# Choosing each token's expert inside the attention loop, and a DRAM list of token numbers in place of a table made at its end

## The chip, the cores and the metric

The kernel runs on one core of one Trainium2 chip. The metric is the device time in microseconds of one execution. A time of 1403.3 us is the median of three runs of the kernel before; the profile is of one more execution.

## What is computed

Eight batches of 512 tokens with 256 channels go through three steps: a cross-attention with 16 heads on 64 context rows, of which each token keeps the 32 highest scores per head; a self-attention with 16 heads of 16 channels; and a feed-forward layer in which each token uses one of eight experts, the one with the highest gate logit. Cut to what the change touches, the last step is:

```python
hn2 = _layernorm(x, ln2_g, ln2_b).reshape(-1, h)
logits = hn2 @ gate_w + gate_b
idx = jnp.argmax(logits, axis=-1)                 # one expert of 8 for each of 4096 tokens
mid = jax.nn.relu(jnp.einsum('th,ehf->etf', hn2, w1) + b1[:, None, :])
y = jnp.einsum('etf,efh->eth', mid, w2) + b2[:, None, :]
moe = y[idx, jnp.arange(hn2.shape[0])]
return x + moe.reshape(b, s, h)
```

## The kernel before

**Two blocks.** The first block is the attention of all eight batches, each in four tiles of 128 tokens (`NT = 4`, `TILES = 32` in all). The second is the routing and the experts: the tokens are sorted by expert into 39 tiles of 128 (`ETILES`), enough for any split of 4096 tokens over eight experts. Between the blocks all engines meet at a barrier.

**The order in the first block.** Each engine's work is written as many small streams (one function for each step of a batch, a tile or a group of heads). `weave` puts the streams of an engine into one order by their due times, which `due(b, kind, n)` works out from the table `AT`: a kind of step, its times within a batch, stretched and shifted for each batch. Batches overlap; the gate of batch b ends while the heads of batch b+1 run. The eight PSUM banks are handed out in the same way: a step that writes an `fr` bank (four of them) takes the next turn in `FR_TURN`, and its turn waits until the reader of the turn four before it is done.

**The places named below.** TensorE's matmuls all go through the helper at L613, its transposes through L616. VectorE finds a bound of each row's scores at L1244 (`nmax`, from scores in `fr` and what ScalarE left in `over`); TensorE transposes `nmax` (`fr<-ident,nmax`, kind `ct`), and ScalarE's exponentials (`pt<-fr`, L1013) follow on scores `fr<-qs,ks`. For the top 32 of the cross-attention VectorE builds `nhi`, `lo`, `merged` and `thr` and the mask `m` (L1180); GpSimd multiplies it with the exponentials (`m<-m,e`, L1358), adds halves, VectorE sums (L1187) and inverts (`rden`, L1201), GpSimd scales (`m<-m,rden`, L1372), and TensorE transposes the product (`xs<-ident,m`). GpSimd also adds a bias (`xy<-xy,bo_b`, L1395) and writes the normalised rows (`row<-xyf,z`, L1413), which go to the DRAM list `rows_d`. The gate is four matmuls for a tile (`fr<-gw,znT`) and VectorE's sum into `logits` (L1293).

**The second block.** The SP queue loads constants (`dcon`, L1472). VectorE then finds the best expert of all 32 tiles at once (L1488 to L1493); two matmuls (L1592, L1593) count the tokens ahead of each; VectorE adds up over the tiles, finds the tile in which each expert begins, each token's slot, and for each slot its tile and row (L1497 to L1551), all on 128 partitions; 32 matmuls (L1628) bring the token numbers into the order of the slots. From `rec` VectorE copies three index columns for each tile into `gix`: the token rows, the weight rows and the `b2` rows. GpSimd fetches by them with indirect DMAs (L1662), two tiles ahead: `rows`, `w1s`, `w2s` and `b2s`. A tile is then two transposes (L1599), 32 matmuls of layer one (L1609), 16 of layer two (L1621), and an indirect DMA of the result (L1700). Weights of an expert that is already in the buffer are not fetched again: their index lies outside the bound.

Of the kernel before, what the change touches and what calls it, by code (L numbers as in the profile page):

```python
# [13 lines left out]
P = 128  # L14
# [21 lines left out]
for _name, _n in (("temp", HP), ("ln1_g", KT), ("ln1_b", KT), ("bq", KT), ("bk", KT), ("bv", KT),  # L36
# [157 lines left out]
FR_TURN = turns("proj", "v", "fs", "ct", "st", "ot", "oT", "wo", "zT", "gt")  # L194
# [28 lines left out]

DCON = {}
for _name, _n in (("before", P), ("ones", P), ("order", E), ("steps", TILES), ("starts", SEGS + 1),
                  ("tile", ETILES), ("row", P), ("part", 1), ("token", TILES)):
    DCON[_name] = sum(n for _, n in DCON.values()), _n
# [8 lines left out]
def program(nc, x, ctxT, maskb, wqT, wk, wv, wo, cols, fwq, fwk, fwv, fwo, bo, gate_w, gate_b,  # L236
            w1b, w2t, b2, ident_in, dcon_in, out):
    ctx = ExitStack()
    with ctx:
# [18 lines left out]
        rows_d = dram("rows_d", (TOK + 1, 2 * DM))  # L258

# [4 lines left out]
        mask_u = sb("mask_u", [P, B * CK], U8)  # L264
# [6 lines left out]
        logits = sb("logits", [P, TILES * E])  # L271
        zrow = sb("zrow", [NT * 4, P])

        def cv(name, n):
            return col[:, COLS[name][0] + n:COLS[name][0] + n + 1]

# [65 lines left out]
        row = sa("row", [P, 2, 2 * DM])  # L342
        znT = sa("znT", [P, KT, P])


        pre_ctx = pt[:, 0, 0:KT, :]
# [46 lines left out]
        rows_stored, scratch_set = [sem(f"rows_stored{n}") for n in range(2)], sem("scratch_set")  # L393

        dcon_loaded = sem("dcon_loaded")
        d_step, oh_ready, count_full, counts_read = sem("d_step"), sem("oh_ready"), sem("count_full"), sem("counts_read")
        rows_ready, tokens_full, rec_ready = sem("rows_ready"), sem("tokens_full"), sem("rec_ready")
# [4 lines left out]
        gix_ready = pair("gix_ready")  # L402
        rows_in, w1_in, w2_in, b2_in = pair("rows_in"), pair("w1_in"), pair("w2_in"), pair("b2_in")
# [44 lines left out]
        def _(sp):  # L448
# [13 lines left out]
            load(mask_u[:, :], maskb.to_broadcast((P, B * CK)), early_loaded)  # L462
# [8 lines left out]
            load(gb_b[:, :], gate_b.to_broadcast((P, E)), const_loaded)  # L471

# [138 lines left out]
        def _(pe):  # L611
# [240 lines left out]
            def gate(b, t):  # L852
# [3 lines left out]
                for k in range(KT):  # L856
                    ins = mm(o[:, 0:E], znT[:, k, :], gw[:, k, :], k == 0, k == KT - 1)
                ins.then_inc(fr_full, 1)

            weave([first_values(), context()]  # L860
                  + [part(b) for b in range(B) for part in (fold_k, fold_v, projections, values)]
# [7 lines left out]
        def _(act):  # L869
# [170 lines left out]
            def out_turned(b, t):  # L1040
                yield due(b, "to", t)
                fr_written(act, b, "oT", t)
                for k in range(KT):
# [410 lines left out]
        def dc(name):  # L1454
            a, n = DCON[name]
            return dcon[:, a:a + n]
# [296 lines left out]
```

## Time and profile before

| | us |
|---|---|
| median of three runs | 1403.3 (1400.73 to 1408.4) |
| the profiled execution | 1396.75 |
| its span, first to last instruction | 1394.9 |
| TensorE busy | 1283.2 (92%) |
| VectorE busy | 942.8 (68%) |
| ScalarE busy | 854.2 (61%) |
| GpSimd busy | 682.3 (49%) |

The busy shares are means over two different blocks, so they tell little by themselves. The attention fills the span up to some 1052 us, the routing the next 37 us, the expert tiles the rest. How full an engine is where a step is to be added is read from the busy time of short stretches, what a step waits for from the timeline.

### The profile page before, as it was taken

Reading aid. Unit: us, or ns where it says so; the run is one execution under the profiler, and the core shown is the slowest. Engines: PE = TensorE matmul, PEld = TensorE weight load, DVE = VectorE, ACT = ScalarE, POOL = GpSimd, SP = SyncE. Lnnn points to the kernel's source line nnn. Section 1 sums busy time; section 2 is a strip of 40 time slices with the busy share of each in tenths; the row PEclk is TensorE's granted clock in tenths of the full one; section 3 lists DMA queues with packets and bytes.
Section 4 is the critical chain, followed back from the end, with each engine's and each line's share of the span. In section 5 each row is a group of like instructions: output and inputs, shape, how many; then the busy total and the mean of one; then the engine's idle time right before and its main releaser. Section 6 shows DMA issues by size and latency. Waiting matters only on the chain. (4 is left out here: it accounts for less than half of the span.)

```text
span 1394.9 us, 27066 instructions
## 1 busy us (share of the span) xinstructions
PE 1283.2 (92%) x7138; PEld 922.0 (66%) x7138; DVE 942.8 (68%) x6185; ACT 854.2 (61%) x2061; POOL 682.3 (49%) x816
## 2 busy tenths in 40 slices
PE   7868799999999999999999999999972899999996
PEld 5445576577576566656757666655531799989996
DVE  3887987996997998799699789944426122222221
ACT  2334488697878879779787887977860122222221
POOL 2557453555356355445624734632013466666673
PEclk9989999999999999999999999999995899999998
DMA  5210641743363184175337417418513264385551
GB/s 189 83 62 9 167 93 31 169 99 77 101 154 82 55 181 93 40 154 121 77 91 155 91 33 196 78 49 195 93 46 136 77 221 152 82 303 187 188 193 26
DMA packets 105009, 161.43 MB, mean 116 GB/s; under 512 B 35058, under 2 KB 58232, under 8 KB 100760
## 3 DMA queue, kind: packets, MB, share of 16 engines
q1 hardware_dynamic: 86760, 106.51, 32.7%
q0 software_dynamic: 18096, 53.19, 11.7%
q8 instruction: 58, 0.95, 0.3%
q14 instruction: 95, 0.78, 0.2%
HBM read 161.81 MB, written 46.53 MB: 149 GB/s over the span
## 5 line engine op out<-in xcount | busy, mean ns | idle before, releaser
L1013 ACT ACTIVATE pt<-fr 128x512 f32<-128x512 f32 x512 | 277.1, 617 | 25.7 <-PE fr L613 22.6
L1244 DVE CUSTOM_DVE_ANT_0 over<-fr,over 128x256 f32<-128x256 f32 x512 | 197.8, 418 | 86.7 <-ACT over L1023 79.2
L1023 ACT ACTIVATE over<-fr 128x256 f32<-128x256 f32 x512 | 179.0, 391 | 53.4 <-PE fr L613 49.0
L613 PE MATMUL fr<-qs,ks 128*128 128x512 f32 x512 | 189.1, 452 | 3.8 <-DMA qs<-cT 1.3
L613 PE MATMUL fr<-ks,qs 128*128 128x256 f32 x512 | 170.7, 352 | 8.1 <-DVE nmax L1244 3.9
L1358 POOL TENSOR_TENSOR m<-m,e 128x1024 f32<-128x1024 f32 x32 | 75.9, 2371 | 185.0 <-DVE m L1180 185.0
L613 PEld LDWEIGHTS fr<-qs,ks 128*128 128x128 f32 x512 | 87.1, 188 | 86.5 <-issue 50.5
L613 PE MATMUL fr<-kd,qs 128*128 128x256 f32 x512 | 137.5, 283 | 0.0
L814 PE MATMUL ob<-pt,v 128*32 128x512 f32 x1024 | 136.4, 604 | 0.6 <-ACT pt L1013 0.5
L613 PEld LDWEIGHTS fr<-ks,qs 128*128 128x128 f32 x512 | 97.8, 191 | 43.9 <-DVE nmax L1244 25.0
L613 PE MATMUL xs<-VW,pT 128*128 128x256 f32 x512 | 120.2, 389 | 1.8 <-issue 1.7
L613 PE MATMUL xs<-M,xnT 128*128 128x512 f32 x256 | 120.3, 592 | 0.2 <-ACT xnT L872 0.2
L613 PEld LDWEIGHTS xs<-VW,pT 128*128 128x128 f32 x512 | 98.9, 196 | 16.2 <-issue 2.3
L613 PEld LDWEIGHTS fr<-kd,qs 128*128 128x128 f32 x512 | 98.4, 192 | 8.0 <-issue 4.8
L1350 POOL TENSOR_TENSOR e<-s,mx 128x1024 f32<-128x1024 f32 x32 | 60.9, 1904 | 62.5 <-issue 36.9
L1157 DVE MAX8 lo<-lo 128x8 f32<-128x32 f32 x512 | 90.3, 177 | 0.0
L1151 DVE MAX8 lo<-lo 128x8 f32<-128x32 f32 x512 | 89.8, 176 | 0.0
L1158 DVE MAX8 nh<-nhi 128x8 f32<-128x32 f32 x512 | 89.6, 175 | 0.0
L1152 DVE MAX8 nh<-nhi 128x8 f32<-128x32 f32 x512 | 89.3, 175 | 0.0
L1155 DVE MATCH_REPLACE8 nhi<-nh,nhi 128x32 f32<-128x32 f32 x512 | 89.0, 174 | 0.0
L1154 DVE MATCH_REPLACE8 lo<-lo 128x32 f32<-128x32 f32 x512 | 88.8, 174 | 0.0
L1372 POOL TENSOR_TENSOR m<-m,rden 128x1024 f32<-128x1024 f32 x32 | 60.9, 1905 | 47.2 <-DVE rden L1201 47.2
(211 smaller groups left out, 2903.9 us busy)
## 6 DMA issues: line engine op xcount, KB each, us to landing
parts_d<-parts SPq DMA_DIRECT2D x32, 512.0 KB, 4.2
ks<-parts_d SPq DMA_DIRECT2D x128, 128.0 KB, 4.0
qs<-parts_d SPq DMA_DIRECT2D x128, 128.0 KB, 4.3
xy_d<-xy SPq DMA_DIRECT2D x32, 256.0 KB, 3.9
kd<-diff_d SPq DMA_DIRECT2D x128, 64.0 KB, 4.1
xyf<-xy_d SPq DMA_DIRECT2D x32, 256.0 KB, 4.0
rows_d<-row SPq DMA_DIRECT2D x32, 256.0 KB, 3.3
diff_d<-diff SPq DMA_DIRECT2D x16, 256.0 KB, 2.3
```

The source lines that it names most:

```text
L613: return pe.matmul(o, l, r, start=first, stop=last)
L814: ins = pe.matmul(ob[VC * h:VC * h + VC, :], v32[:, t, 4 * g + h, :], pt[:, t % 2, h, :], start=(t == 0), stop=(t == NT - 1))
L1013: act.activation(pt[:, t % 2, h, :], fr_bank(b, "st", 16 * g + n)[:, :], ACT.Exp, scale=D ** -0.5)\
L1023: act.activation(over[:, (16 * g + n + 64 * b) % NREL, :], fr_bank(b, "fs", 16 * g + n)[:, S // 2:S], ACT.Relu)\
L1151: v.max(lo17[:, h, 1:9], lv[:, h, :])
L1152: ins = v.max(nh17[:, h, 0:8], nv[:, h, :])
L1154: v.match_replace(lv[:, h, :], lo17[:, h, 1:9], lv[:, h, :], -BIG)
L1155: ins = v.match_replace(nv[:, h, :], nh17[:, h, 0:8], nv[:, h, :], -BIG)
L1157: v.max(lo17[:, h, 9:17], lv[:, h, :])
L1158: ins = v.max(nh17[:, h, 8:16], nv[:, h, :])
L1244: v.tensor_tensor_reduce(rest, fr_bank(b, "fs", 16 * g + n)[:, 0:S // 2], rest, 1.0, -BIG, ALU.add, ALU.max, nmax[:, g % 2, 4 * h + t:4 * ...
L1358: gp.tensor_tensor(m[:, :, :], m[:, :, :], e[:, :, :], ALU.mult).then_inc(em_ready, 1)
```

## The change

**Choice and count, batch by batch.** `choose` finds the expert of the batch's 512 tokens once their logits are there (ties go to the lower number), in five steps on 128x32; `places` has TensorE count by five matmuls the tokens of the same expert ahead of each token: in the tile, in earlier tiles of the batch, and in earlier batches (`acc`); `count` adds the batch to `acc`; `slots` picks each token's place, as an integer. Each expert owns a region of 4096 places in the list. `ids_out` scatters the token numbers of a tile to their places in a DRAM list `ids_d`, with an indirect DMA of 128 numbers of 4 bytes, four for each batch. The list is filled with the number 4096 (no token) ahead of time.

**The second block.** It counts on 8 partitions how many tiles each expert needs, makes a table of 39 tiles by matmuls, and one indirect DMA fetches the 39 rows of 128 token numbers. One transpose turns them into `row_table`; `w_table` holds the weight rows. GpSimd's DMAs take their indices from the two tables, so that the copies into `gix` and `sid` go. `b2` stands behind the rows of `w2` (2304 words), so that the `b2` DMA goes. The first tile is always of expert 0, and its weights are plain loads on the SP queue at the block's start. The sum with the residual rows (`resb`) moves on VectorE behind the middle layer. The constants are loaded in the prologue.

The new kinds in the table, and the new streams (`mm` is the matmul helper, `fr_slot` takes the bank's turn):

```diff
+    "ch": (331.237,),
+    "dp": (333.413,),
+    "cn": (333.871,),
+    "sx": (335.219,),
+    "ro": (338.117, 339.873, 341.639, 343.291),
-FR_TURN = turns("proj", "v", "fs", "ct", "st", "ot", "oT", "wo", "zT", "gt")
+FR_TURN = turns("proj", "v", "fs", "ct", "st", "ot", "oT", "wo", "zT", "gt", "dp")
...
+            def places(b):
+                yield due(b, "dp")
...
+                pe.wait_ge(oh_ready, b + 1)
+                wait(pe, acc_ready, b)
+                o = fr_slot(b, "dp", 0)
+                chosen_here = oh[:, :, :].rearrange("p t e -> p (t e)")
+                mm(o[:, 0:NT * E], earlier[:, :], chosen_here, True, False)
+                mm(o[:, 0:NT * E].rearrange("p (t e) -> p t e", e=E), ones[:, :],
+                   acc[:, b % 2, :].unsqueeze(1).to_broadcast((P, NT, E)), False, False)
+                for back in range(1, NT):
+                    ins = mm(o[:, back * E:NT * E], ones[:, :], chosen_here[:, 0:(NT - back) * E], False, back == NT - 1)
+                ins.then_inc(fr_full, 1)
...
+            def set_picks():
+                yield due(0, "nx", 0) - 0.01
+                dve.wait_ge(dcon_loaded, 16 * 3)
+                v.tensor_copy(earlier[:, :], oT[:, 0, :])
+                v.tensor_copy(ones[:, :], oT[:, 1, :])
+                v.tensor_copy(acc[:, 0, :], znT[:, 0, 0:E]).then_inc(pick_set, 1)
+
+            def choose(b):
+                yield due(b, "ch")
...
+                v.tensor_reduce(best[:, :], logits[:, :, :], AX.X, ALU.max).then_inc(choice_step, 1)
+                dve.wait_ge(choice_step, 4 * b + 1)
+                v.tensor_tensor(ow[:, :, :], logits[:, :, :], best[:, :].unsqueeze(2).to_broadcast(wide), ALU.is_ge)\
+                 .then_inc(choice_step, 1)
...
+                v.tensor_tensor(oh[:, :, :], ow[:, :, :], best[:, :].unsqueeze(2).to_broadcast(wide), ALU.is_equal)\
+                 .then_inc(oh_ready, 1)
...
+            def slots(b):
+                yield due(b, "sx")
+                fr_written(dve, b, "dp", 0)
+                v.tensor_tensor(ow[:, :, :], fr_bank(b, "dp", 0)[:, 0:NT * E].rearrange("p (t e) -> p t e", e=E),
+                                oh[:, :, :].bitcast(F32), ALU.mult).then_inc(fr_signal(b, "dp", 0), 1)
...
+            def ids_out(b):
+                for t in range(NT):
+                    yield due(b, "ro", t)
...
+                    if t == 0:
+                        pool.wait_ge(slots_ready, b + 1)
+                    pool.sem_inc(p_gate, 1)
+                    gp.indirect_dma_start(ids_d.rearrange("r (p o) -> (r p) o", o=1),
+                                          bass.IndirectOffsetOnAxis(slot_i[:, t:t + 1], 0),
+                                          dc("token")[:, b * NT + t:b * NT + t + 1], None,
+                                          bounds_check=E * REGION - 1, oob_is_err=False).then_inc(ids_stored, 16)
```

The second block, cut to its core:

```diff
-            sp.dma_start(dcon[:, :], dcon_in).then_inc(dcon_loaded, 16)
+            sp.dma_start(w1s[:, 0, :], w1b[0:P, :]).then_inc(first_w1, 16)
+            sp.dma_start(w2s[:, 0, :], w2t[0:P, :]).then_inc(first_w2, 16)
...
+            settle(v.tensor_scalar(cnt[:, :], counts_at[:, 0:1], of_expert("region"), None, ALU.subtract))
+            settle(v.tensor_scalar(more_than[:, :], of_expert("steps"), cnt[:, 0:1], None, ALU.is_lt))
+            v.tensor_reduce(need[:, :], more_than[:, :], AX.X, ALU.add).then_inc(need_ready, 1)
...
+            dve.wait_ge(table_full, 1)
+            v.tensor_scalar(ids_at[:, :], begins_at, 1.0 / P, dc("part")[0:ETILES, :], ALU.mult, ALU.add)\
+             .then_inc(ids_at_ready, 1)
...
+            dve.wait_ge(ids_full, 1)
+            v.tensor_copy(row_table[:, :], ids_t).then_inc(ids_ready, 1)
...
+            pe.transpose(ids_t, ids[:, :], ident[0:ETILES, 0:ETILES]).then_inc(ids_full, 1)
...
-            for t in range(TILES):
-                if t % 8 == 0:
-                    pe.wait_ge(rows_ready, t // 8 + 1)
-                ins = pe.matmul(EO[1][:, 0:SEGS], at_row[:, t, :], at_tile[:, t, :], start=(t == 0),
-                                stop=(t == TILES - 1))
...
-            for q in range(2):
-                pool.wait_ge(gix_ready[q], 1)
-                fetch_w1(0, q)
-                fetch_w2(0, q)
+            pool.wait_ge(ids_at_ready, 1)
+            pool.wait_ge(ids_stored, 16 * TILES)
+            gather(ids[:, :], ids_d, ids_at[:, :], ids_in, RTILES - 1)
+            pool.wait_ge(tables_ready, 1)
+            fetch_w1(0, 1)
+            pool.wait_ge(ids_ready, 1)
             for q in range(2):
                 fetch_rows(0, q)
+            fetch_w2(0, 1)
```

**Where the new steps stand.** On TensorE, where the gate of batch 0 has just ended; `xs<-kbd,wqT_s` is a fold of keys, `ob<-pt,v` the values under the exponentials. Before:

```order
L613 MATMUL fr<-kd,qs 128x256
L613 MATMUL fr<-qs,ks 128x512 x3
L613 MATMUL xs<-kbd,wqT_s 128x128 x4
L616 MATMUL fr<-ident,nmax 16x128
L613 MATMUL fr<-qs,ks 128x512 x4
L814 MATMUL ob<-pt,v 32x512 x4
```

After:

```order
L645 MATMUL fr<-kd,qs 128x256
L645 MATMUL fr<-qs,ks 128x512 x3
L645 MATMUL xs<-kbd,wqT_s 128x128 x4
L648 MATMUL fr<-ident,nmax 16x128
L645 MATMUL fr<-oh,earlier 128x32
L645 MATMUL fr<-acc,ones 128x32
L645 MATMUL fr<-oh,ones 128x24
L645 MATMUL fr<-oh,ones 128x16
L645 MATMUL fr<-oh,ones 128x8
L645 MATMUL fr<-qs,ks 128x512 x4
L846 MATMUL ob<-pt,v 32x512 x4
```

The five counting matmuls stand between the transpose of `nmax` and the next scores for ScalarE.

On VectorE at the same place; `ISA` is the top-key step that gives `nmax`. Before:

```order
L1121 SCALAR_TENSOR_TENSOR nhi<-s,nb 128x512
L1244 ISA over,nmax<-fr,over 128x256
L1244 ISA nmax 128x1
L1172 TENSOR_REDUCE thr<-merged 128x16
L1128 TENSOR_TENSOR lo<-s 128x512
L1180 TENSOR_TENSOR m<-s,thr 128x1024
```

After:

```order
L1170 SCALAR_TENSOR_TENSOR nhi<-s,nb 128x512
L1358 TENSOR_REDUCE best<-logits 128x4
L1360 TENSOR_TENSOR ow<-logits,best 128x32
L1363 TENSOR_TENSOR ow<-ow,dcon 128x32
L1366 TENSOR_REDUCE best<-ow 128x4
L1371 TENSOR_TENSOR oh<-ow,best 128x32
L1293 ISA over,nmax<-fr,over 128x256
L1293 ISA nmax 128x1
L1221 TENSOR_REDUCE thr<-merged 128x16
L1378 TENSOR_REDUCE tsum<-oh 128x8
L1381 TENSOR_TENSOR acc<-acc,tsum 128x8
L1177 TENSOR_TENSOR lo<-s 128x512
```

The choice's five steps stand ahead of that step, the count's two ahead of `lo`; the slots' three steps and then `m` follow. (Batches 3 and 5 have the choice ahead of `nhi`, batch 2 the slots ahead of `lo`.)

On GpSimd, behind batch 0's gate. Before:

```order
L1350 TENSOR_TENSOR e<-s,mx 128x1024
L1413 TENSOR_TENSOR row<-xyf,z 128x256
L1372 TENSOR_TENSOR m<-m,rden 128x1024
L1395 TENSOR_TENSOR xy<-xy,bo_b 128x256
L1358 TENSOR_TENSOR m<-m,e 128x1024
L1364 TENSOR_TENSOR e<-e 128x16x32
L1366 TENSOR_TENSOR e<-m 128x16x32
```

After:

```order
L1449 TENSOR_TENSOR e<-s,mx 128x1024
L1512 TENSOR_TENSOR row<-xyf,z 128x256
L1524 DMA ids_d<-dcon,slot_i 37760x1
L1471 TENSOR_TENSOR m<-m,rden 128x1024
L1524 DMA ids_d<-dcon,slot_i 37760x1
L1494 TENSOR_TENSOR xy<-xy,bo_b 128x256
L1524 DMA ids_d<-dcon,slot_i 37760x1 x2
L1457 TENSOR_TENSOR m<-m,e 128x1024
L1463 TENSOR_TENSOR e<-e 128x16x32
```

The four scatters stand around `m<-m,rden` and ahead of the next `m<-m,e`; batches 1 to 5 read alike. Batch 6's four stand together between two pairs of `row` steps, batch 7's behind its last `row`, ahead of the barrier.

At the end of the first block on GpSimd, from the last `row` over the barrier (the branches). Before:

```order
L1413 TENSOR_TENSOR row<-xyf,z 128x256 x2
L1422 UNCONDITIONAL_BRANCH
L1656 UNCONDITIONAL_BRANCH
L1662 DMA w1s<-w1b,gix 128x2056
L1662 DMA w2s<-w2t,gix 128x2048
L1662 DMA b2s<-b,gix 128x256
L1662 DMA w1s<-w1b,gix 128x2056
```

After:

```order
L1512 TENSOR_TENSOR row<-xyf,z 128x256 x2
L1524 DMA ids_d<-dcon,slot_i 37760x1 x4
L1535 UNCONDITIONAL_BRANCH
L1718 UNCONDITIONAL_BRANCH
L1724 DMA ids<-ids_d,ids_at 39x128
L1724 DMA w1s<-w1b,w_table 128x2056
L1724 DMA rows<-rows_d,row_table 128x512 x2
L1724 DMA w2s<-w2t,w_table 128x2304
```

Four scatters stand ahead of the barrier, and behind it the fetch of the token numbers comes first.

## Rows read from the trace of the kernel before

**Rows 1.** By stretch: length; busy PE, PEld, DVE, ACT, POOL; granted clock, DMA.
```profile
297.70:306.00 8.30, 8.30 (x54) 5.27 (x53) 8.30 (x56) 7.98 (x19) 7.60 (x10) 1.00 0.63 90
306.00:317.80 11.80, 11.80 (x73) 7.49 (x72) 11.13 (x97) 11.08 (x23) 6.12 (x5) 1.00 0.36 65
1052.50:1077.00 24.50, 2.07 (x4) 1.17 (x4) 18.74 (x50) 0.00 (x0) 7.88 (x5) 0.50 0.32 107
```

**Rows 2.** Timeline of the gap: start us, length us, engine, operation, [idle before].
```profile
1051.71 0.17 DVE L1293 TENSOR_TENSOR logits<-fr,gb_b 128x8 f32<-128x8 f32 x1 [2.07 <-PE fr L613]
1052.17 0.34 SPq L1472 DMA_DIRECT2D dcon<-dcon_in  x1
...
1072.63 0.19 DVE L1545 SCALAR_TENSOR_TENSOR best<-best,slot 128x32 f32<-128x32 f32 x1
1072.86 0.35 DVE L1546 TENSOR_SCALAR best<-best 128x32 f32<-128x32 f32 x1
...
1084.87 0.21 DVE L1557 TENSOR_SCALAR gix<-rec 128x1 uint32<-128x1 f32 x2
1085.88 1.00 POOL L1662 DMA_INDIRECT rows<-rows_d,gix  x1 [7.45 <-DVE gix L1557]
...
1089.29 0.69 PE L1599 MATMUL fr<-ident,rows 128*128 128x128 f32 x2 [4.71 <-DMA rows<-rows_d,gix]
```

**Rows 3.** Timeline of the loop, where the gate of batch 0 ends.
```profile
297.06 0.51 PE L613 MATMUL fr<-gw,znT 128*128 128x8 f32 x4
...
299.12 1.05 PE L613 MATMUL xs<-kbd,wqT_s 128*128 128x128 f32 x8
...
299.55 0.08 DVE L1244 DVE_READ_ACCUMULATOR2_ANT nmax<- 128x1 f32 x1
...
300.01 0.27 PE L616 MATMUL fr<-ident,nmax 128*16 128x128 f32 x1
```

**Rows 4.** Timeline of the gap, GpSimd's first six indirect DMAs.
```profile
1067.90 1.36 POOL L1662 DMA_INDIRECT w1s<-w1b,gix  x1 [18.36 <-issue]
...
1069.57 2.34 POOL L1662 DMA_INDIRECT w2s<-w2t,gix  x1 [0.31 <-issue]
...
1072.21 1.01 POOL L1662 DMA_INDIRECT b2s<-b,gix  x1 [0.30 <-issue]
...
1073.52 2.07 POOL L1662 DMA_INDIRECT w1s<-w1b,gix  x1 [0.30 <-issue]
...
1075.89 1.22 POOL L1662 DMA_INDIRECT w2s<-w2t,gix  x1 [0.30 <-issue]
...
1077.42 1.00 POOL L1662 DMA_INDIRECT b2s<-b,gix  x1 [0.30 <-issue]
```

**Rows 5.** Expert tiles: chain of waits; last, TensorE's waits (us, times, longest).
```profile
1090.88 5.47 PE xs L1609 x32
...
1100.02 3.57 PE fr L1609 x32
...
1127.51 5.67 DMA rows<-rows_d,gix
...
PE fr L1599 <- DMA rows<-rows_d,gix: 5.1, 5, 1.5
```

**Rows 6.** Timeline of GpSimd, and last of VectorE, behind batch 0's gate.
```profile
310.99 0.73 POOL L1413 TENSOR_TENSOR row<-xyf,z 128x256 f32<-128x256 f32 x1
312.59 1.90 POOL L1372 TENSOR_TENSOR m<-m,rden 128x1024 f32<-128x1024 f32 x1 [0.87 <-DVE rden L1201]
314.45 0.73 POOL L1395 TENSOR_TENSOR xy<-xy,bo_b 128x256 f32<-128x256 f32 x1
319.14 2.38 POOL L1358 TENSOR_TENSOR m<-m,e 128x1024 f32<-128x1024 f32 x1 [3.95 <-DVE m L1180]
...
324.26 1.22 DVE L1187 TENSOR_REDUCE sums<-e 128x32 f32<-128x1024 f32 x1 [2.62 <-POOL e L1366]
```

**Rows 7.** Waits from 297.7 to 414.7: us in total, times, longest.
```profile
PEld xs L616 <- POOL m L1372: 1.1, 2, 0.9
```

More of the change, by code:

```diff
@@ L221 @@
 W1COLS = KT * FF + FT
+REGION = TOK
+RTILES = E * REGION // P + ETILES
+W2COLS = FT * DM + DM
 DCON = {}
-for _name, _n in (("before", P), ("ones", P), ("order", E), ("steps", TILES), ("starts", SEGS + 1),
-                  ("tile", ETILES), ("row", P), ("part", 1), ("token", TILES)):
+for _name, _n in (("order", E), ("token", TILES), ("part", 1), ("upto", E), ("steps", TILES),
+                  ("tile", ETILES), ("bump", 1), ("region", 1), ("expert", 1)):
     DCON[_name] = sum(n for _, n in DCON.values()), _n
@@ L270, in program @@
         gw = sb("gw", [P, KT, E])
-        logits = sb("logits", [P, TILES * E])
+        dcon = sb("dcon", [P, NDCON])
+        earlier = sb("earlier", [P, P], F32R)
+        ones = sb("ones", [P, P], F32R)
+        acc = sb("acc", [P, 2, E], F32R)
         zrow = sb("zrow", [NT * 4, P])
@@ L1042, in out_turned @@
                 fr_written(act, b, "oT", t)
+                if b == 0 and t == 0:
+                    act.wait_ge(pick_set, 1)
                 for k in range(KT):
@@ L1298, in _ @@
+            weave([place_keys(), set_picks()]
+                  + [part(b) for b in range(B) for part in (x_stats, parts_low, choose, count, slots)]
                   + [part(b, t) for b in range(B) for t in range(NT)
@@ L1554, in _, with of_expert @@
[L1554 to L1565 removed]
+            def of_expert(name):
+                return dc(name)[0:E, :]
@@ new lines, in _ @@
+            settle(v.tensor_tensor(begins[:, :], starts_at, need[:, :], ALU.subtract))
+            v.tensor_scalar(weigh[:, :], begins[:, :], -float(P), of_expert("region"), ALU.mult, ALU.add)
+            settle(v.tensor_scalar(is_under[:, :], of_expert("tile"), ends[:, :], None, ALU.is_lt))
+            settle(v.scalar_tensor_tensor(chosen[:, :], of_expert("tile"), begins[:, :], is_under[:, :], ALU.is_ge, ALU.mult))
+            v.tensor_scalar(numbered[:, :], chosen[:, :], of_expert("expert"), None, ALU.mult).then_inc(chosen_ready, 1)
@@ L1723 @@
     w2 = np.asarray(L0_ffn_w2).reshape(E, FT, P, DM).transpose(0, 2, 1, 3).reshape(E * P, FT * DM)
+    w2 = np.concatenate([w2, np.repeat(np.asarray(L0_ffn_b2), P, axis=0)], axis=1)
+    token = np.arange(P)[:, None]
+    experts = np.arange(P)[:, None] % E
     dcon = np.zeros((P, NDCON), np.float32)
-    for name, value in (("before", np.triu(np.ones((P, P)), 1)), ("ones", 1.0), ("order", E - np.arange(E)),
-                        ("steps", P * np.arange(TILES)), ("starts", P * np.arange(SEGS + 1)),
-                        ("tile", np.arange(ETILES)), ("row", np.arange(P)),
-                        ("part", np.arange(P)[:, None]),
-                        ("token", P * np.arange(TILES)[None, :] + np.arange(P)[:, None] - TOK)):
+    for name, value in (("order", E - np.arange(E)), ("token", token + P * np.arange(TILES)), ("part", token),
+                        ("upto", experts <= np.arange(E)),
+                        ("steps", np.where(np.arange(TILES) == 0, -1, P * np.arange(TILES))),
+                        ("tile", np.arange(ETILES)), ("bump", np.where(experts == E - 1, ETILES, 0)),
+                        ("region", REGION * experts), ("expert", experts)):
         a, n = DCON[name]
         dcon[:, a:a + n] = value
+    pick = np.concatenate([np.triu(np.ones((P, P)), 1), np.ones((P, P)),
+                           np.tile(REGION // P * np.arange(E), (P, 1))], axis=1).astype(np.float32)
     arrays = {
```

248 lines of the change are left out of this document (119 added, 129 removed).

## The prediction

> **What bounds the kernel now.** I read the busy time by stretch first, since a kernel of two blocks has more than one limit. Inside the attention loop (I use the turn of some 117 us that begins at 297.7 us) TensorE, VectorE and ScalarE are all full in the first 8.3 us, and nearly full in the next 11.8; between the blocks, from 1052.5 to 1077 us, TensorE works 2 us of 24.5, at half clock [rows 1]. So there is one long part where a stall of TensorE is paid in full, and one gap of which every microsecond lies on the path that ends the kernel.
>
> The timeline of that gap gives its length: the last logits are written at 1051.71 + 0.17 = 1051.88 us, and the first transpose of the expert tiles starts at 1089.29 [rows 2]. That is 37.4 us, nearly all of it a chain of VectorE's steps; behind it 39 expert tiles run at their own pace. The profiled execution took 1396.75 us (span 1394.9) and the median of the three runs is 1403.3, so 6.55 us are added to a sum made on the trace before it is compared with the median.
>
> **The change part by part: the gap.** It loses the 128-partition chain, the 32 matmuls on `at_tile` and the load of the constants; it gains the last batch's choice, four scatters ahead of the barrier, a short chain, and a fetch of the numbers.
> - Choice of batch 7: five dependent VectorE steps. Two such steps on 128x32 start 0.23 us apart [rows 2], so 1.15 us, to 1053.0. Five small matmuls: the gate's four take 0.51 us in the loop [rows 3], so 0.6 to 0.9, to 1053.8. Three steps for the slots, 0.7, to 1054.5.
> - GpSimd starts an indirect DMA about 0.8 us after the VectorE step that releases it (1084.87 + 0.21 to 1085.88) [rows 2]. Four scatters at 1.00 us, its price with VectorE quiet [rows 2], with 0.30 between them [rows 4], take 4.9: 1055.3 to 1060.2. Then the barrier, 0.3 us by the first DMA issue behind the last logits (1051.88 to 1052.17) [rows 2]: 1060.5.
> - The table on 8 partitions: some ten VectorE steps at 0.2, and three passes through TensorE at about 0.4 (an estimate: the nmax transpose takes 0.27 [rows 3], the rest is the hop there and back): 3.3 us, to 1063.8. GpSimd starts 0.8 later. The fetch lands 3.4 us after its start if it goes as the first row fetch did (1085.88 to 1089.29) [rows 2], or 5.7 to 5.9 if it queues behind weights, as the one of 5.67 us did [rows 5]; the SP queue is loading 2.2 MB of first weights beside it (128 rows of 2056 and of 2304 words). So 1068.0 to 1070.5.
> - Transpose and conversion 0.5, GpSimd 0.8, row fetch again 3.4 to 5.9: the first transpose stands at 1072.7 to 1077.7, in the middle 1075.2. **The gap shrinks by 11.6 to 16.6 us; I take 14.1.**
> - The first layer of the first tile took 5.47 us, against 3.57 for the same work later [rows 5]. The 32 matmuls that kept TensorE at work just ahead of it are gone, so the slow part may last into the second layer: 0 to 3 us more, I take 1. In the tiles one of five GpSimd DMAs goes (the `b2` rows), and TensorE's waits for late rows, 5.1 us in five places [rows 5], may get shorter: 0 to 3 us less, I take 1. These two cancel. That the row fetch now waits for the residual sum, which moves behind the middle layer, is counted in these bounds.
>
> **The change part by part: the loop.** For batches 0 to 5 the new work falls into the full stretch.
> - Choice ahead of nmax. In batch 0 the choice stands on VectorE between `nhi` and the top-key step that gives nmax; that ended at 299.55 + 0.08 = 299.63 us, and TensorE, coming from its folds, transposed nmax at 300.01 [rows 3]. That is a cover of some 0.35 us for a delay of 1.15: TensorE stalls 0.8. Queued behind on TensorE are the scores that feed ScalarE's exponentials, and ScalarE is full there too [rows 1].
> - `dp`: five matmuls at the gate's price (0.51 us for four [rows 3]) are 0.6 us more on TensorE; 0.4 if their loads overlap, at most 1.
> - VectorE gets ten steps in all, some 2.2 us, in a stretch where it idles 0.67 us of 20.1 [rows 1]. TensorE's own shift of 1.4 and these 0.67 cover that nearly.
> - GpSimd: one scatter goes on each side of `m<-m,rden`, and two right ahead of `m<-m,e`, which started at 319.14 after 3.95 us of idle time [rows 6]. In a frame that shifts with TensorE: the first scatter 312.1 to 313.1, `m<-m,rden` to 315.1, the second scatter 315.4 to 316.4, `xy` to 317.2, the others 317.5 to 319.8, so that `m<-m,e` starts at 319.9 in place of 319.14. The chain from there is tight: VectorE waits 2.62 us for its sums [rows 6], and TensorE's weight load waits for the product at its end, 1.1 us in two places of a turn [rows 7]. So 0.75 us come on top at 1.00 us a scatter, and each further 0.1 us of a scatter adds 0.4.
> - **A turn: 0.8 + 0.6 + 0.75 = 2.15 us, six times 12.9.** Batch 6's set lies where GpSimd is idle; 0.4 for its steps on TensorE and VectorE. The three copies of `set_picks`, 0.4. The loads added to the prologue lie behind larger ones: nothing, at most 0.5. Together **13.7 us**.
>
> Total: -14.1 + 13.7 = -0.4, so 1396.4 us for a profiled execution and **1403 us** against the median: no change that shows. (About 0.5%, 7 us, is what a measurement of this kernel can tell from none.)
>
> **A rule against the change.** The six DMAs that GpSimd issued beside VectorE's long steps took 1.36, 2.34, 1.01, 2.07, 1.22 and 1.00 us [rows 4], the one with VectorE quiet 1.00 [rows 2]. The Trainium skill (SBUF — State Buffer, section "SBUF: two separate sides") gives a mechanism: VectorE's two-port operations hold a port pair that GpSimd needs to write its descriptors, and a DMA of some 620 ns took some 3100 ns beside a copy. By that ratio, as an estimate, four scatters would cost 16 us more a turn, not 0.75. The rows agree in direction and show far less.
>
> **The rivals.**
> - *The stalls are absorbed* (faster). TensorE's busy time has modelled ends, so part of its 100% can be waiting, and VectorE's wait of 2.62 us [rows 6] shows slack behind the insertion. If the other engines catch up while TensorE stalls, only `dp` and some 0.2 us of the rest stay: 0.8 a turn, 4.8 + 0.8 in all. Then -14.1 + 5.6 = -8.5: 1395 us. Against it: ScalarE is full in the same stretch [rows 1], and can't catch up with work that comes late.
> - *GpSimd's scatters are dear* (slower). At 1.5 us, the mean of the six [rows 4], `m<-m,e` moves 2.0 us further on the tight chain: 4.15 a turn, 24.9 + 0.8 - 14.1 = +11.6: 1415 us. It decides (more than 7 us above) from about 1.3 us a scatter. For it: VectorE is at 94% from 306 to 317.8 [rows 1]. Against it: beside the six stood VectorE's widest steps of the chain, which the loop doesn't have there. The port rule above is this case at its largest.
> - *The gap gives less* (within 0.5%). If the fetch of the numbers and that of the rows both queue behind the first weights, the gap shrinks by 10 in place of 14: 1407 us.
>
> **How the numbers follow.** The forecast with the third rival: 0.45, own range 1396 to 1410. Absorbed: 0.28, 1389 to 1396. Dear scatters: 0.27, 1410 to 1425. The range leaves out one in ten at either end: 1389 to 1419. Faster 0.28, same 0.45, slower 0.27.
>
> **What would show it.** In the trace after: the first transpose some 23 us behind the last logits in place of 37.4; turns of the six batches 2.1 us longer; a wait of the nmax transpose of about 0.8 us once a turn; `m<-m,e` right behind the scatters, without idle time; scatters of 1.0 us each. Turns less than 1 us longer speak for the absorbed case; scatters above 1.3 us, with TensorE waiting for GpSimd's product, for the dear one. The prediction is wrong at its root if the first transpose comes later than 30 us behind the logits, or if TensorE waits microseconds for the choice ahead of the five matmuls.

## The result, and the profile after

The changed kernel takes **1437.1 us** (median of 4 runs, 1431.4 to 1440.5) beside 1405.9 for the kernel before in the same comparison: a ratio of **1.0216**, 95% interval 1.0184 to 1.0249. It is slower by some 31 us, and the time lies 18 us above the upper end of the range.

| | before | after |
|---|---|---|
| profiled execution | 1396.75 | 1433.84 |
| its span | 1394.9 | 1431.5 |
| last logits start at | 1051.71 | 1099.48 |
| last logits written to first transpose of the tiles | 37.4 | 28.8 |
| first transpose to the end | 305.6 | 303.0 |

So the second block and the gap got 11.2 us shorter, and the loop 47.8 us longer. TensorE's row of the page, in 40 slices, doesn't show it: the loop is as full as before (first row before, second after).

```profile
PE   7868799999999999999999999999972899999996
PE   7868799999998999999999999998895499999997
```

What shows it is the waits over the whole loop, from 296 to 1100 us (engine, line, whom it waited for: us in total, times, longest). VectorE waits for the input rows `xb`, a wait that the trace of before doesn't list at all, and TensorE's waits for `nmax` grow:

```profile
DVE xstat L1144 <- DMA xb<-x: 11.8, 4, 4.1
PE fr L645 <- DVE nmax L1293: 18.7, 30, 3.3
PE fr L648 <- DVE nmax L1293: 8.8, 16, 1.5
```

The same rows of the kernel before, from 290 to 1052 us:

```profile
PE fr L613 <- DVE nmax L1244: 7.3, 25, 0.4
PE fr L616 <- DVE nmax L1244: 3.4, 9, 0.5
```

**The place, in batch 0.** GpSimd first: the rows that answer to [rows 6]. The scatters take about the 1.0 us they were priced at, and `m<-m,e` follows them without idle time.

```profile
318.69 1.24 POOL L1524 DMA_INDIRECT ids_d<-dcon,slot_i  x1 [0.18 <-issue]
319.96 1.92 POOL L1471 TENSOR_TENSOR m<-m,rden 128x1024 f32<-128x1024 f32 x1
322.05 1.01 POOL L1524 DMA_INDIRECT ids_d<-dcon,slot_i  x1 [0.17 <-issue]
...
324.00 0.99 POOL L1524 DMA_INDIRECT ids_d<-dcon,slot_i  x1 [0.17 <-issue]
325.30 0.97 POOL L1524 DMA_INDIRECT ids_d<-dcon,slot_i  x1 [0.31 <-issue]
326.29 2.40 POOL L1457 TENSOR_TENSOR m<-m,e 128x1024 f32<-128x1024 f32 x1
```

The damage is on another queue. The SP queue, the VectorE step that uses its load, and TensorE behind that (the timeline of the same stretch):

```profile
322.39 0.39 SPq L528 DMA_DIRECT2D xb<-x  x1
...
326.13 4.99 SPq L591 DMA_DIRECT2D kd<-diff_d  x4
...
330.48 0.75 DVE L1144 BATCH_NORM_STATS2 xstat<-xb 128x6 f32<-128x256 f32 x2 [4.10 <-DMA xb<-x]
...
331.95 0.79 PE L645 MATMUL fr<-qs,ks 128*128 128x512 f32 x1 [3.32 <-DVE nmax L1293]
332.55 4.89 PE L645 MATMUL xs<-VW,pT 128*128 128x256 f32 x11
```

`xb` is issued while the scatters are on their way and lands 8.1 us later. VectorE works in order, so it stands 4.10 us at the row statistics, and the `nmax` step queued behind them comes late; TensorE idles 3.32 us. Behind that its clock is lower: from 332 to 340 us the granted clock is 0.65 in the mean (below; columns as in [rows 1]), that is 0.50 (1.2 GHz) until 337.6 us and then 1.00 again (2.4 GHz), where the same matmuls of the kernel before ran at 1.00. That nearly doubles the price: batch 0 loses 6.1 us here, batches 1 and 2 5.1 and 4.8.

```profile
332.00:340.00 8.00, 8.00 (x28) 6.27 (x32) 2.57 (x8) 1.63 (x5) 5.40 (x11) 0.65 0.24 38
```

The landing times of the SP queue's transfers and of the scatters in this stretch (318 to 332 us: queue, operation, times, KB each, median us to landing) name the partner:

```profile
qs<-parts_d SPq DMA_DIRECT2D x4, 128.0 KB, 9.2
xb<-x SPq DMA_DIRECT2D x1, 256.0 KB, 8.1
xy_d<-xy SPq DMA_DIRECT2D x1, 256.0 KB, 11.6
kd<-diff_d SPq DMA_DIRECT2D x4, 64.0 KB, 8.6
ids_d<-dcon,slot_i POOLq DMA_INDIRECT x4, 10.2
```

In the kernel before the same four landed sooner (312 to 326 us):

```profile
qs<-parts_d SPq DMA_DIRECT2D x4, 128.0 KB, 4.3
xb<-x SPq DMA_DIRECT2D x1, 256.0 KB, 3.0
xy_d<-xy SPq DMA_DIRECT2D x1, 256.0 KB, 4.4
kd<-diff_d SPq DMA_DIRECT2D x4, 64.0 KB, 3.4
```

The four scatters move 2 KB in all. (`xy_d<-xy` is a store, the other three are loads.)

**The gap.** The steps go as worked out, but for one hole (the rows that answer to [rows 2]):

```profile
1099.48 0.17 DVE L1343 TENSOR_TENSOR logits<-fr,gb_b 128x8 f32<-128x8 f32 x1 [2.27 <-PE fr L645]
...
1103.68 1.09 POOL L1524 DMA_INDIRECT ids_d<-dcon,slot_i  x1 [7.20 <-DVE slot_i L1393]
...
1107.62 0.97 POOL L1524 DMA_INDIRECT ids_d<-dcon,slot_i  x1 [0.30 <-issue]
1115.68 0.34 SPq L1586 DMA_DIRECT2D w1s<-w1b  x1
...
1119.76 1.02 POOL L1724 DMA_INDIRECT ids<-ids_d,ids_at  x1 [11.17 <-DVE ids_at L1619]
...
1128.48 0.69 PE L1667 MATMUL fr<-ident,rows 128*128 128x128 f32 x2 [4.52 <-DMA rows<-rows_d,row_table]
```

The last scatter is started by 1108.59, and the second block's first instruction comes at 1115.68: the barrier costs 7.1 us, not 0.3. The four scatters, with no other packet on the queues (1100 to 1116 us), land after 5.3 us in the median; the last of them lands at 1114.08, 1.6 us ahead of that instruction.

```profile
ids_d<-dcon,slot_i POOLq DMA_INDIRECT x4, 5.3
```

### The profile page after: what moved, and what is told of

Its sections match the earlier page's. It is cut to its first block and busy times, and to the rows that moved or that the text cites. A ratio compares the mean times of both kernels' runs of the same rounds, so it can differ in the third digit from the quotient of the medians.

```text
span 1431.5 us, 27019 instructions
## 1 busy us (share of the span) xinstructions
PE 1300.1 (91%) x7150; PEld 929.3 (65%) x7150; DVE 931.4 (65%) x6152; ACT 856.1 (60%) x2061; POOL 669.4 (47%) x808
## 5 line engine op out<-in xcount | busy, mean ns | idle before, releaser
L645 PE MATMUL fr<-qs,ks 128*128 128x512 f32 x512 | 190.0, 456 | 13.9 <-DVE nmax L1293 11.2
L645 PE MATMUL fr<-ks,qs 128*128 128x256 f32 x512 | 170.0, 351 | 13.7 <-DVE nmax L1293 4.7
L645 PE MATMUL xs<-VW,pT 128*128 128x256 f32 x512 | 125.4, 402 | 1.8 <-issue 1.7
L645 PE MATMUL xs<-M,xnT 128*128 128x512 f32 x256 | 124.1, 608 | 0.2 <-ACT xnT L919 0.2
L645 PEld LDWEIGHTS xs<-VW,pT 128*128 128x128 f32 x512 | 102.6, 203 | 17.9 <-issue 2.3
L1206 DVE MAX8 lo<-lo 128x8 f32<-128x32 f32 x512 | 93.0, 183 | 0.0
L1200 DVE MAX8 lo<-lo 128x8 f32<-128x32 f32 x512 | 92.8, 182 | 0.0
L1201 DVE MAX8 nh<-nhi 128x8 f32<-128x32 f32 x512 | 92.4, 181 | 0.0
L1207 DVE MAX8 nh<-nhi 128x8 f32<-128x32 f32 x512 | 92.3, 182 | 0.0
L1204 DVE MATCH_REPLACE8 nhi<-nh,nhi 128x32 f32<-128x32 f32 x512 | 92.2, 180 | 0.0
L1203 DVE MATCH_REPLACE8 lo<-lo 128x32 f32<-128x32 f32 x512 | 92.0, 180 | 0.0
```

The source lines that it names most:

```text
L645: return pe.matmul(o, l, r, start=first, stop=last)
L1200: v.max(lo17[:, h, 1:9], lv[:, h, :])
L1201: ins = v.max(nh17[:, h, 0:8], nv[:, h, :])
L1203: v.match_replace(lv[:, h, :], lo17[:, h, 1:9], lv[:, h, :], -BIG)
L1204: ins = v.match_replace(nv[:, h, :], nh17[:, h, 0:8], nv[:, h, :], -BIG)
L1206: v.max(lo17[:, h, 9:17], lv[:, h, :])
```

## The experiments

The table gives how far TensorE is behind the kernel before, in us: the start of a matmul less the start of the same matmul in the trace of before, at four places, and how much the six turns between the first two add. The last column is the gap from the last logits to the first transpose (37.4 before). Each row is one profiled execution; `e3_quiet` and `e5_quiet_behind`, which have the same loop, differ by 1.5 us in the six turns and by 3.7 at the last logits. The first column is read at 285 us of the kernel before; from there to the choice at 299 us TensorE makes up 0.8 to 1.1 us in every kernel, so that the six turns cost that much more than the column shows.

| kernel | ahead of the first choice | six turns | 930 to 985 us | batch 6 | at the last logits | gap |
|---|---|---|---|---|---|---|
| after | 5.8 | +27.4 | +3.7 | +6.7 | 47.8 | 28.8 |
| `e1_last_only` | 6.1 | +11.7 | +5.4 | 0 | 27.1 | 28.8 |
| `e2_late_stats` | 3.9 | +20.9 | +3.8 | +5.9 | 37.2 | 28.6 |
| `e3_quiet` | 0.5 | +12.2 | +5.8 | +7.2 | 29.2 | 28.8 |
| `e5_quiet_behind` | 1.2 | +10.7 | +3.2 | +6.1 | 25.5 | 25.8 |
| `e6_far` | 5.8 | +19.1 | +4.8 | 0 | 34.0 | 29.3 |
| `e7_rows512` | 5.1 | +15.4 | +5.4 | 0 | 30.0 | 29.4 |
| `e8_all_moved` | 7.2 | +12.6 | +4.3 | 0 | 28.9 | 25.0 |
| `e9_clear_of_pool` | 7.3 | +20.1 | +3.6 | 0 | 36.7 | 25.5 |
| `e10_weights_after` | 4.9 | +19.9 | +5.9 | 0 | 36.5 | 27.7 |
| `e11_count_later` | 3.4 | +3.1 | +5.0 | 0 | 17.5 | 26.5 |

In the last four rows batch 6's choice and count stand later than the column "batch 6" reaches; they cost another 1.3 to 2.2 us there. The rest up to the last logits, 2.6 to 4.3 us in every row, falls at the end of the loop.

**The scatters of batches 0 to 6 left out** (`e1_last_only`):

```diff
+                    if b < B - 1:
+                        continue
```

> The changed kernel without the scatters of batches 0 to 6 (choice, count and slots stay; most tokens are not in the list, so the expert tiles work on empty rows and only the first block's time is read). In the changed kernel the last logits lie 47.8 us later than before: 5.8 before batch 0's choice, 1.4 at each choice, and 1.5 to 6.6 behind each group of scatters. Theory A, the scatters' traffic slows the loads of the SP queue: the load of xb lands in some 3 us again, VectorE no longer waits for it, only the 1.4 us a batch stay, and the last logits lie 9 to 16 us later than before. Rival B, the ten VectorE steps take the load's slack: the waits for xb stay at 3 to 4 us in batches 0 to 2, and the logits lie 40 us or more later.

1411.3 us (one run), 22.6 below the profiled run of after. VectorE's wait for `xb` falls to 0.6 us, and the stalls of batches 0 to 2 and 6 are gone; about 1.4 us a turn stay at the choice and the five matmuls.

```profile
DVE xstat L1144 <- DMA xb<-x: 0.6, 1, 0.6
```

So the scatters cost 20.7 us of the loop's 47.8, and the rival falls. But the logits are still 27.1 us late, where the theory asked for 9 to 16: what is left without any scatter is larger than the 1.4 us a batch. The account below comes back to it.

**The statistics of `xb` some 6 us later on VectorE** (`e2_late_stats`):

```diff
-    "st_x": (-15.912, 3.065)
+    "st_x": (-10.0, 3.065)
-    "xf": (-13.465, -0.981)
+    "xf": (-8.5, -0.981)
```

> The changed kernel with VectorE's row statistics of xb (and GpSimd's step on them) some 6 us later in the order, behind the sums; scatters as they are. Theory A with the wait in VectorE's order as its way to TensorE: the load still lands in 7 to 8 us, but nobody waits for it; the stalls of 3 us on nmax and the half-clock stretch behind them go in batches 0 to 2, some 15 us less in all. If instead the late loads of qs and kd carry the loss, TensorE waits for those at the same places and the time moves by less than 5 us. Rival B expects the same gain as A, so this run tells only the way, not the cause.

1421.5 us (one run), 12.3 below the profiled run of after, where some 15 were expected. VectorE no longer waits for `xb`, and the stalls of batches 0 to 2 shrink from 6.1, 5.1 and 4.8 to 2.7, 4.8 and 1.5 us; batch 6 keeps 5.9. The load lands as late as before (up to 9.0 us). In batches 0 and 1 what is left begins with the next late transfer on the same queue: VectorE's sum `xy<-xs,xb` reuses a buffer whose store `xy_d<-xy`, issued at 322.01, lands at 334.39.

```profile
334.47 0.42 DVE L1257 TENSOR_TENSOR xy<-xs,xb 128x256 f32<-128x256 f32 x1 [2.96 <-issue]
```

So the way to TensorE is a wait in VectorE's order, but not for `xb` alone: taking that wait away saves 6.5 us of the 15.7 that the scatters cost in the six turns.

**The scatters some 35 us later** in GpSimd's order, where the SP queue has nothing to load (`e3_quiet`):

```diff
-    "ro": (338.117, 339.873, 341.639, 343.291),
+    "ro": (374.0, 375.0, 376.0, 377.0),
```

> The changed kernel with the scatters of every batch some 36 us later in GpSimd's order, where the trace of before shows GpSimd idle for 17 us and next to no DMA traffic; nothing else moved. Theory A: the scatters collide with no load, the stalls of 3 to 6.6 us go, the loop loses 1.4 us a batch and the whole takes 20 to 30 us less than the changed kernel, some 1407 to 1415. Rival B: within 5 us of the changed kernel, 1432 or more.

1417.4 us (1414.5 to 1420.5), ratio 1.0083 (1.0060 to 1.0107), a little above the 1407 to 1415 that were expected. The six turns fall from 27.4 to 12.2. Batch 6 got no better, because its scatters didn't move: in both kernels GpSimd has been idle for 12.7 us there and starts them 1.2 us behind the slots. They meet `ks`, `qs` and `kd` of the last batch, and the picture of batch 0 repeats, with TensorE six microseconds idle.

```profile
1006.59 0.97 POOL L1524 DMA_INDIRECT ids_d<-dcon,slot_i  x1 [0.30 <-issue]
...
1009.73 5.01 SPq L591 DMA_DIRECT2D kd<-diff_d  x4
...
1018.58 0.55 PE L645 MATMUL fr<-ks,qs 128*128 128x256 f32 x1 [6.00 <-issue]
```

The quiet place doesn't make the scatters quick. A scatter's landing adds 16 counts to its semaphore, four scatters 64, and the trace holds the times of most of these. In batches 0 to 5 the last count comes 6.5 to 14.9 us after the start of the fourth scatter, in the change 7.5 to 12.8. What the quiet place saves is the transfers beside them.

**What of a scatter slows the others?** Two kernels keep the scatters of batches 0 to 6 where the change has them. `e6_far` writes the same 4 bytes to places 512 B apart; `e7_rows512` writes 512 B to each of those places (the edit of the first; its slots are multiplied by 128 as well):

```diff
+        far_d = dram("far_d", (RTILES * P, P))
...
+                    gp.indirect_dma_start(ids_d.rearrange("r (p o) -> (r p) o", o=1) if last else far_d.rearrange("r (p o) -> (r p) o", o=1),
```

> The changed kernel, with the scatters of batches 0 to 6 at their places in GpSimd's order, each still 128 numbers of 4 bytes, but to places 512 bytes apart in a larger list (the rows of those batches are then missing from the real list, so only the first block's time is read). The scatters of the changed kernel land after 6.7 us (median) and up to 12.8, the xb load beside them after 8. If neighbouring addresses are the cause (many 4-byte writes into the same short piece of memory), the scatters land in about 3 us, the xb load too, and the last logits move from 47.8 to some 27 us behind the kernel before. If it is the size of each write, or their number, nothing changes by more than 5 us.

> As the run before, but each of the 128 pieces is a row of 512 bytes, one per place of 512 bytes: the same number of pieces, none of them small (again only the first block's time is read). If the small size of the writes is the cause, they land in about 3 us, as the result rows of the expert tiles do (2.4 us, 128 pieces of 1 KB), the xb load in 3, and the logits lie some 27 us behind the kernel before. If the number of pieces is the cause, it behaves like the changed kernel, at 40 us or more.

1419.0 and 1415.0 us. In `e6_far` the same stretch of batch 0 reads as in the kernel before:

```profile
qs<-parts_d SPq DMA_DIRECT2D x4, 128.0 KB, 3.7
xb<-x SPq DMA_DIRECT2D x1, 256.0 KB, 2.8
xy_d<-xy SPq DMA_DIRECT2D x1, 256.0 KB, 3.1
kd<-diff_d SPq DMA_DIRECT2D x4, 64.0 KB, 3.4
far_d<-dcon,slot_i POOLq DMA_INDIRECT x4, 4.3
```

In this run the spread scatters land after 3.6 us in the median (2.1 to 5.6) at the crowded place of the loop, the four of the last batch, still side by side, after 4.4 to 6.4 with idle queues. The number of pieces is the same in all three (128 for each scatter), so it isn't the number. Small writes to neighbouring addresses land late themselves and hold up the loads beside them; spread out, they cost 34.0 - 27.1 = 6.9 us, and as larger pieces 2.9, where the expectation was no cost in either. Why the landing of the neighbouring writes differs from batch to batch (6.5 to 14.9 us in `e3_quiet`) was not tried. What in the memory or the DMA engines does it, these runs don't tell. The Trainium skill (DMA: Bandwidth & Descriptors, section "Specifications") says that below 512 B a transfer is done as a read-modify-write. By that rule alone `e6_far`, still at 4 bytes, would have kept the cost, and it kept a third of it; only the 4 us between `e6_far` and `e7_rows512` fit it, and those are single runs. Whether pieces within the same 512 B have to wait for one another is not told apart here.

**The last batch's scatters behind the barrier**, with the quiet place (`e5_quiet_behind`):

```diff
+            pool.wait_ge(slots_ready, B)
+            for t in range(NT):
+                scatter_ids(pool, B - 1, t)
             pool.wait_ge(ids_at_ready, 1)
```

> As the run before, and the last batch's four scatters issued behind the barrier in place of ahead of it. In the changed kernel GpSimd's drain at the end of the first block lasts until 1115.45 us, 6.9 us past its last scatter's descriptors. If the drain waits for the landing of the scatters, the barrier passes some 12 us earlier relative to the logits, the fetch of the numbers waits for the landing in place of it, and the gap from the last logits to the first transpose goes from 28.8 to 23 to 25 us: 4 to 6 us less than the run before. If the drain is something else (a fixed price of an engine that has used indirect DMAs), it stays as long, and the gap grows by the scatters' 5 us.

1412.5 us (10 runs), ratio 1.0053 (1.0030 to 1.0076). The gap is 25.8 us in place of 28.8, just outside the 23 to 25 that were expected. The slots end at 1080.52, and the second block begins 0.3 us behind them. The hole of 7 us is gone from the barrier, and most of it is back as a wait for the same scatters ahead of the fetch:

```profile
1080.80 0.34 SPq L1589 DMA_DIRECT2D w1s<-w1b  x1
...
1085.56 0.98 POOL L296 DMA_INDIRECT ids_d<-dcon,slot_i  x1 [0.30 <-issue]
1095.48 1.03 POOL L1727 DMA_INDIRECT ids<-ids_d,ids_at  x1 [8.94 <-issue]
```

So the barrier waits for the landing. In all six kernels with the last scatters ahead of it the next block begins 1.6 us after their last count (0.5 in `e1_last_only`), in the five with them behind it 0.3 us after the slots.

**The choice and the count later too** (`e8_all_moved`), some 22 us (the five matmuls 28) behind their place in the change:

```diff
-    "ch": (331.237,),
-    "dp": (333.413,),
+    "ch": (353.037,),
+    "dp": (361.037,),
```

> The kernel with the scatters in the quiet stretch and the last four behind the barrier, and besides: choice and count stand on VectorE ahead of the sums of the next cross-attention tile, where it waited 2.62 us for GpSimd; the five matmuls some 8 us behind them; slots where VectorE waited 2.8 us for ScalarE. If the 1.4 us that TensorE loses at each choice are 0.8 for nmax and 0.6 for the matmuls, the first part goes and 0.5 to 0.6 a batch stay, 5 us less in all; batch 6's scatters come some 20 us later, behind the loads with which they collided (7 us less). Together 8 to 12 us under the 1412.5 of the run it is built on, so some 1402, level with the kernel before or a little under. If moving the choice doesn't help, 1405 to 1410.

1408.8 us (12 runs), ratio 1.0045 (1.0021 to 1.0069): not the 1402 that was expected, and not clearly better than the run it is built on (1.0053). Nothing is lost at the old place any more (6.4 us behind at 299 and at 318 us), but 1 to 5 us in each turn at the new one. VectorE and GpSimd there:

```profile
327.97 1.28 POOL L1470 TENSOR_TENSOR e<-e 128x512 f32<-128x512 f32 x1
329.33 1.26 POOL L1472 TENSOR_TENSOR e<-m 128x512 f32<-128x512 f32 x1
...
328.15 1.15 DVE L1367 TENSOR_TENSOR ow<-logits,best 128x32 f32<-128x32 f32 x1
329.34 1.31 DVE L1370 TENSOR_TENSOR ow<-ow,dcon 128x32 f32<-128x32 f32 x1
```

Two VectorE steps of 0.19 us take 1.15 and 1.31, and end with the GpSimd steps beside them. The one-input step between such steps (`best`) stays at 0.19.

**Clear of GpSimd's long steps** (`e9_clear_of_pool`: the choice 10 us later again, the matmuls at 366), and the same with the first weights held until the list is complete (`e10_weights_after`):

```diff
-    "ch": (353.037,),
-    "dp": (361.037,),
+    "ch": (362.737,),
+    "dp": (366.000,),
```

```diff
+            sp.wait_ge(ids_stored, 16 * TILES)
             sp.dma_start(w1s[:, 0, :], w1b[0:P, :]).then_inc(first_w1, 16)
```

> The kernel with everything moved, once more with the choice and the count some 10 us later on VectorE, behind GpSimd's product and half sums, where VectorE had 3.09 us of idle time at 338.84 and GpSimd worked only on pieces one element wide; the five matmuls and the slots follow, the scatters stay in the quiet stretch. If VectorE's two-input steps were held by GpSimd's long ones (1.15 and 1.31 us where 0.19 is usual, ending with them), the five steps take 0.2 us each again, and TensorE loses the 1.1 to 1.5 us at the weight load of the product in batches 0 to 4 and most of the 5.1 us at batch 4: some 9 us less, 1400 us by the runs of that kernel (median 1408.8). If the steps are long for another reason (their operands, the logits just written), they are long here too, and the time stays at 1409.

> The same, and the SP queue's 2.2 MB of first weights start only when all token numbers are in the list. In the kernel with everything moved, GpSimd had started the last scatter at 1088.99 and waited 8.16 us until 1098.12 before it could fetch the numbers; in the loop scatters land after 3.1 us. If the weights' traffic held them, the fetch starts some 5 us sooner and lands sooner too, and the gap from the last logits to the first transpose is some 20 us in place of 25, 4 to 5 us less than the other kernel of this call, unless the first layer then waits for its weights (1.05 MB; at some 200 GB/s 5 us, with 8 us to go). If the scatters of one batch need 8 us by themselves when four follow each other, the wait stays and the weights come late: 5 to 10 us more.

In `e9_clear_of_pool` the steps are short again in all eight batches (shortest, median and longest, ns), which fits the reason given. That the logits had just been written is not it: in the change the steps stand right behind the logits and take 191 to 194 ns.

```profile
L1367 DVE TENSOR_TENSOR ow<-logits,best x8: 191/192/194, 337.9 to 1088.9; 128x32 f32<-128x32 f32 x8
```

The time is not shorter: 1416.6 us, ratio 1.0081 (1.0058 to 1.0104), where 1400 was expected. The matmuls take a turn of the four `fr` banks, and at their new place that bank's last reader was not done; behind the idle time the clock falls again (0.72 in the mean from 342 to 348 us, 0.50 from 343 to 346).

```profile
340.52 0.42 DVE L1300 CUSTOM_DVE_ANT_0 over<-fr,over 128x256 f32<-128x256 f32 x1 [1.32 <-ACT over L1077]
...
341.10 0.25 PE L652 MATMUL fr<-oh,earlier 128*128 128x32 f32 x1 [1.86 <-DVE nmax L1300]
```

`e10_weights_after` took 1419.7 us, ratio 1.0108 (1.0084 to 1.0132). With nothing else on the queues GpSimd still waited 6.64 us behind its last scatter (8.72 in `e9_clear_of_pool`), so the four scatters need most of that by themselves:

```profile
1104.21 1.03 POOL L1728 DMA_INDIRECT ids<-ids_d,ids_at  x1 [6.64 <-issue]
```

That agrees with the landing in the loop as read above. The 3.1 us of the expectation were read wrongly: they are the landing of the list's first filling and of the fetch, which use the same list, and of no scatter. The fetch of the numbers then lies beside the weights and takes 7.0 us in place of 2.3: the gap is 27.7 us in place of 25.5.

**The matmuls some 6 us later on TensorE** (369 in place of 366 in the table), where the bank has long been read (`e11_count_later`):

```diff
-    "dp": (366.000,),
+    "dp": (369.000,),
```

> The kernel with the choice clear of GpSimd once more, with the five counting matmuls some 6 us later on TensorE, behind `xs<-VW,pT`, the last `osb` transposes and an nmax transpose; VectorE's slots stay where they are. In the kernel of before this one TensorE stood at those matmuls for 1.86 us, since they take a turn of the `fr` banks whose reader, VectorE's nmax, came at 340.87; behind them it ran `xs<-VW,pT` at half clock, and the bank was held until the slots read it at 348.69: 2.3 to 4.3 us in each of six batches. If the bank's turn was that cost, these go, since four turns before the new place the bank has been read for 3 us: some 18 us less of 1416.6, that is 1399, the first version at or below the kernel before (1404). If the cost is the five matmuls' wait for the choice, whatever the place, or the choice's place on VectorE, the time stays near 1416.

**1400.4 us** (12 runs, 1395.1 to 1404.6) beside 1404.6 for the kernel before: ratio **0.9968** (0.9949 to 0.9988). This version is 0.3% faster than the kernel before (by the interval 0.1 to 0.5%), and by the two ratios 2.4% faster than the change. (Its profiled execution is 3.6 us longer than that of before, which lies 8 us under this median.) The matmuls start without a wait, the granted clock from 330 to 348 us is 1.00, and six turns cost 3.1 us in all.

```profile
340.87 0.58 PE L652 MATMUL fr<-oh,earlier 128*128 128x32 f32 x1
...
336.00:342.00 6.00, 6.00 (x32) 4.62 (x31) 3.32 (x16) 3.25 (x10) 2.20 (x8) 1.00 0.26 84
342.00:348.00 6.00, 6.00 (x32) 4.60 (x32) 4.78 (x20) 4.54 (x16) 2.60 (x7) 1.00 0.02 8
```

## Why the prediction was wrong

**The gap: right but for the scatters' landing.** The choice, the matmuls and the slots of batch 7 end at 1102.81, 3.2 us behind the logits (forecast 2.6); four scatters take 4.9 us as forecast; from the barrier to the first transpose it is 12.8 us, inside the 12.2 to 17.2 of the steps. What was wrong is the barrier's 0.3 us. It was read from a place where GpSimd had no DMA under way [rows 2]; behind four scatters it took 7.1 us, since it waits for their landing. The sum had no term for that landing, and needed one wherever the barrier stands: the fetch can't start before the list is complete, and with the scatters behind the barrier it waited 6.64 to 9.55 us for them. The gap shrank by 8.6 us in place of 14.1.

**The tiles: right in sum.** The first layer took 5.21 us (5.47 before [rows 5]), and the tiles are 2.6 us shorter in all, where I took nothing.

**The choice and the matmuls in the loop: right.** 0.8 + 0.6 = 1.4 us was forecast for a turn; TensorE loses 1.35 to 1.5 us there in each of batches 0 to 5, the first part of it as a wait for `nmax` of 0.62 us in batch 0. A turn without scatters costs more than this, though: 11.7 us for six in `e1_last_only`, 1.95 each. The other half microsecond is lost at places ahead of the next choice and was not followed up.

**The scatters: the step that failed.** I priced a scatter as time on GpSimd, 1.00 us each, and let its bytes cost nothing. The price was right (0.97 to 1.24 us), and so was its effect on the chain behind: `m<-m,e` started 0.85 us later than TensorE's shift alone explains, where 0.75 was forecast. `e7_rows512` and `e6_far` come nearest to that term alone, since they keep the scatters on GpSimd and take most of their traffic's effect away: a turn costs 2.6 and 3.2 us, 0.6 and 1.2 more than without scatters, where 0.75 was forecast. The change's turns cost 4.6. The rest is the term that the sum didn't have: what 512 small writes do to the SP queue's loads in the same microseconds. The working looked at what each new step delays on its own engine, and not at what the queue beside it was loading; yet the DMA column of the very rows I used shows the queues busy at 0.36 to 0.63 just ahead of the scatters [rows 1]. Batch 6, priced at 0.4 us because GpSimd is idle there, lost 6.7: idle on the engine was not idle on the queue. Yet the missing term is not the whole miss. The loop is 34.1 us over its 13.7; the scatters cost 20.7 where 4.5 were priced, which makes some 16 of these, and most of the others lie in the three shares that stay open below. The gap is 5.5 us over, the tiles 2.6 under.

**The rivals.** "Scatters are dear" had the sign right and the mechanism wrong: it asked for scatters above 1.3 us, and they took 1.0. "Absorbed" fell at the choice. The mark set for an error at the root, that the first transpose comes later than 30 us behind the logits, was not met (28.8); what was met was a stall of microseconds, at a place that I hadn't named.

**What stays open.** Three shares of the 47.8 us are not the scatters' or the choice's. TensorE is 5.8 us behind ahead of the first new step. That share is 0.5 to 7.3 us in the variants, none of which changes anything there, and lies in stretches of the prologue at half clock (from 126 to 133 us 0.51 in the kernel after, 1.00 before); the profiled execution of before lies under its median (1396.75 and 1405.9), so part of it may be that. From 930 to 985 us 3.2 to 5.9 us are lost in every variant, also without scatters: a load `xyf<-xy_d`, issued at the same place of the order, lands 7.0 to 9.6 us after its issue, where it took 5.8 before. And 4.2 us (2.6 to 4.3 in the variants) go at a granted clock near one half at the end of the loop (0.57 in `e11_count_later` from 1050 to 1062 us, 1.00 before). Together that is 13.7 us in the change. The causes of the last two were not tried.

## What to carry to other kernels

A DMA has two prices: the time on the engine that issues it, and what its traffic does to transfers beside it. A scatter of a few bytes is cheap by the first and may be dear by the second, so look at what the other queues load in the microseconds behind it, and who in program order stands behind a late load. When steps are moved into free time, "free" must hold on every resource that they take (the engine, the queue, the port, the PSUM bank), which took four moves to find here.

## What the runs showed of the hardware that was not expected

- Indirect writes of 4 bytes to neighbouring DRAM places, 512 pieces in 8 us, slowed unrelated transfers on the SP queue from 3.0 to 4.4 us to 8.1 to 11.6; with the places 512 B apart these took 2.8 to 3.7 us. The neighbouring writes are slow by themselves: with no other traffic (gap of the change) they landed after 5.3 us in the median, and in the quiet stretch (DMA share 0.02, `e3_quiet`) the last count of four came 6.5 to 14.9 us after the fourth one's start. The same pieces 512 B apart landed after 3.6 us in the median, in a crowded stretch.
- A VectorE step with two inputs in SBUF was held until a GpSimd `TENSOR_TENSOR` beside it had ended: 0.19 us became 1.15 and 1.31. The Trainium skill (SBUF — State Buffer, section "Who interferes with whom") says that a DVE instruction with two SBUF inputs contends with a GpSimd instruction that reads SBUF. The trace agrees, and so does the one-input step between, at 0.19. The slowing of GpSimd's DMAs by VectorE that the prediction weighed did not come: 0.97 to 1.24 us in the loop.
- Behind four scatters the barrier between the blocks took 7.1 us, in place of 0.3: it passed 1.6 us after their landing.
- An idle time of TensorE of 3.3 us (the change, batch 0) and of 1.9 us (`e9_clear_of_pool`) cost 2.7 and 1.7 us more behind it, at a granted clock of 0.50 (1.2 GHz), until the clock was back at 1.00.
